# Four-layer network on one core: blocks centred by their weights, row maxima rounded once, new interleaving tables

## Reference

```python
for blk in range(3):
    y = _qlora_linear(h, qweights[i0], scales[i0], biases[i0], lora_a[i0], lora_b[i0])
    y = _layernorm(y, ln_gamma[blk], ln_beta[blk])
    y = gelu(y)
    y = _qlora_linear(y, qweights[i1], ...)
    h = y + h
```

## Time and profile before

| | |
|---|---|
| median of 3 runs | 3338.98 us (3332.05 to 3342.03) |
| profiled execution | 3332.12 us, span 3330.2 us |
| TensorE busy | 2776.6 us, 83%, 20640 products' records |
| ScalarE busy | 1912.7 us, 57% |
| VectorE busy | 1760.9 us, 53% |
| mean granted TensorE clock | 0.851 of 2.4 GHz |
| DMA | 18.83 MB, mean 6 GB/s |

### The profile page before, as it was taken

The page is one execution under the profiler, slowest core; times in us unless marked ns, Lnnn a source line. Parts: engine busy times, 40 slices in busy tenths (PEclk is TensorE's granted clock), DMA queues, the critical chain, the costliest instruction groups (busy, mean ns, idle before and its releaser), DMA issues.

```text
span 3330.2 us, 50269 instructions
## 1 busy us (share of the span) xinstructions
PE 2776.6 (83%) x20640; PEld 1752.4 (53%) x20640; DVE 1760.9 (53%) x2698; ACT 1912.7 (57%) x1963; POOL 3.6 (0%) x13
## 2 busy tenths in 40 slices
PE   7999989778997789977898888987889879897426
PEld 4776556454564545645455554555545545554213
DVE  5464464644656446564555545555455554564425
ACT  2333334875248753587535864468634686347996
POOL 0000000000000000000000000000000000000000
PEclk8998899779997688977999778987779887898558
DMA  3000000000000000000000000000000000000000
GB/s 128 2 1 1 19 2 1 1 1 7 1 1 1 0 8 1 1 1 1 8 2 1 1 1 8 2 1 1 1 4 2 1 1 1 4 1 1 0 0 7
DMA packets 4570, 18.83 MB, mean 6 GB/s; under 512 B 608, under 2 KB 864, under 8 KB 3808
## 3 DMA queue, kind: packets, MB, share of 16 engines
q1 hardware_dynamic: 4320, 15.38, 1.2%
HBM read 13.28 MB, written 2.10 MB: 5 GB/s over the span
## 4 chain that ended last, share of the span: by engine, by line
PE 58%; ACT 19%; DVE 12%; issue 11%; DVEq 0%; DMA 0%; ACTq 0%; SPq 0%
ACT back_cosines L1379 6%; PE two_ps L1934 3%; ACT back_cosines L1381 3%; PE one_ps L918 2%; PE one_ps L1934 2%; PE two_ps L1334 2%; PE one_ps L1220 2%; PE two_ps L966 1%; PE one_ps L1782 1%; PE two_ps L918 1%; ACT L1379 1%; PE one_ps L893 1%; PE two_ps L613 1%; PE one_ps L899 1%; PE one_ps L822 1%
## 5 line engine op out<-in xcount | busy, mean ns | idle before, releaser
L1379 ACT ACTIVATE back_cosines<-back_cosines 128x2048 f32<-128x2048 f32 x256 | 473.3, 1899 | 0.5
L989 ACT ACTIVATE front_scratch<-one_ps 128x1152 f32<-128x1152 f32 x168 | 171.6, 1022 | 230.4 <-PE one_ps L904 230.2
L1934 PEld LDWEIGHTS two_ps<-zero_f,wts 128*128 128x128 f32 x1270 | 210.1, 232 | 114.6 <-issue 90.9
L1934 PE MATMUL two_ps<-zero_f,wts 128*128 128x128 f32 x1270 | 235.2, 327 | 35.1 <-DVE back_cosines L1452 18.1
L1381 ACT ACTIVATE back_cosines<-back_cosines,wts 128x2048 f32<-128x2048 f32 x128 | 252.1, 1994 | 13.3 <-DVE back_cosines L1452 13.1
L853 DVE TENSOR_REDUCE front_negm<-one_ps 128x8 f32<-128x1024 f32 (+1 forms) x168 | 202.5, 1221 | 99.0 <-PE one_ps L828 97.7
L1389 DVE TENSOR_REDUCE back_nsum<-back_cosines 128x8 f32<-128x2048 f32 x64 | 144.4, 2281 | 186.9 <-ACT back_cosines L1379 186.9
L752 ACT ACTIVATE back_cosines<-two_ps,wts 128x512 fp32r<-128x512 f32 x28 | 19.2, 687 | 236.3 <-PE two_ps L966 236.3
L822 PE MATMUL one_ps<-front_qkr 32*128 32x128 f32 (+1 forms) x896 | 117.8, 363 | 42.7 <-issue 34.4
L1452 DVE TENSOR_SCALAR back_cosines<-two_ps 128x2048 f32<-128x2048 f32 x56 | 128.1, 2287 | 30.2 <-PE two_ps L1313 30.1
L989 ACT ACTIVATE back_cosines<-two_ps 128x1152 f32<-128x1152 f32 (+1 forms) x84 | 86.1, 1025 | 98.3 <-PE two_ps L904 98.3
(11 more groups left out here) (635 smaller groups left out, 5941.8 us busy)
## 6 DMA issues: line engine op xcount, KB each, us to landing
wts<-w_dram SPq DMA_DIRECT2D x1, 4184.0 KB, 15.2
front_xin<-x_dram SPq DMA_DIRECT2D x8, 256.0 KB, 4.3
out_dram<-back_z SPq DMA_DIRECT2D x8, 256.0 KB, 2.0
wts<-w_dram SPq DMA_DIRECT2D x1, 1736.5 KB, 19.1
wts<-w_dram SPq DMA_DIRECT2D x1, 1199.0 KB, 5.4
wts<-w_dram SPq DMA_DIRECT2D x1, 1152.0 KB, 16.7
wts<-w_dram SPq DMA_DIRECT2D x3, 256.0 KB, 5.9
wts<-w_dram SPq DMA_DIRECT2D x1, 516.5 KB, 4.5
```

The source lines that it names most:

```text
L989: nc.scalar.activation(h.probs[:, e % 2, 0:n * HEADW].rearrange("p (k c) -> p k c", c=HEADW), h.ps[:, 0:n, 0:HEADW], ACT.Exp, scale=float( ...
L1379: nc.scalar.activation(cosines, cosines, func, scale=scale).then_inc(h.arc_pass.sem, 1)
L1934: nc.tensor.matmul(h.ps[:, bank, quarter * P:(quarter + 1) * P], C("ident"), zero_f[:].broadcast_to([P, P]), start=True, stop=True, skip_g ...
```

## The change

The row maxima are written by the reductions directly in fp32r into the even columns of `negm`. The copies into neighbour columns, the exact two-part split and its constants go. TensorE multiplies each tile by an fp32r identity instead of transposing it in fp32: three tiles after the last reduction but one, the fourth after the last, into a second bank. VectorE copies 384 columns and then 128 into `maxTr`, and the scores wait for the second copy.

In the blocks, the centring is applied to the first linear's weights and bias once, before the loop. ScalarE squares PSUM plus the centred bias, and VectorE's output pass adds that bias and multiplies. The bias add, the centring product and the stage names `block{i}_in` go.

All nine order lists are new. The idle products are placed anew: 91 in a front pass, 96 in a back pass. The load of `qlora` moves ahead of `lora` and the quantised weights and has a semaphore of its own.

The entries of the lists are left out of the diff.

```diff
-    "block0": ("y", "xn", True, "eps5", "block0_in", None),
+    "block0": ("y", "xn", False, "eps5", None, None),
...
-            yield
-            pe.wait_ge(h.max_pair.sem, h.max_pair.at(turn, s))
+            yield from max_end_pe(pe, h, turn, s, MSETS)
+
+        def max_end_pe(pe, h, turn, s, sets):
+            yield
+            pe.wait_ge(h.max_done.sem, h.max_done.at(turn, s, sets - 1))
             for t in range(TILES):
-                last = nc.tensor.transpose(h.ps[:, 0, t * P:(t + 1) * P], h.negm[:, t, :], C("ident"))
-            last.then_inc(h.negm_ps.sem, 1)
+                if t == TILES - 1:
+                    yield
+                    pe.wait_ge(h.max_done.sem, h.max_done.at(turn, s, sets))
+                last = nc.tensor.matmul(h.ps[:, t // (TILES - 1), t % (TILES - 1) * P:(t % (TILES - 1) + 1) * P],
+                                        h.negm[:, t, :], ident_r[:], start=True, stop=True, skip_group_check=True)
+                if t >= TILES - 2:
+                    last.then_inc(h.negm_ps.sem, 1)
...
-        def max_end_dve(dve, h, turn, s, sets):
-            yield
-            dve.wait_ge(h.max_done.sem, h.max_done.at(turn, s, sets))
-            for t in range(TILES):
-                last = nc.vector.tensor_copy(max_columns(h, slice(t, t + 1), 1)[:, 0], max_columns(h, slice(t, t + 1), 0)[:, 0])
-            last.then_inc(h.max_pair.sem, 1)
-            yield
-            dve.wait_ge(h.negm_ps.sem, h.negm_ps.at(turn, s))
-            high_dve(dve, h.ps[:, 0, :], h.high[:, 0, :], "m_sign", h.negm_high)
-            yield
-            dve.wait_ge(h.negm_high.sem, h.negm_high.at(turn, s))
-            split_dve(dve, h.ps[:, 0, :], h.high[:, 0, :], "m_low", h.maxTr[:, :], h.negm_ready)
+        def max_end_dve(dve, h, turn, s):
+            for i, columns in enumerate((slice(0, (TILES - 1) * P), slice((TILES - 1) * P, TOK))):
+                yield
+                dve.wait_ge(h.negm_ps.sem, h.negm_ps.at(turn, s, i + 1))
+                nc.vector.tensor_copy(h.maxTr[:, columns], h.ps[:, i, 0:columns.stop - columns.start]).then_inc(h.negm_ready.sem, 1)
...
-                        pe.wait_ge(h.negm_ready.sem, h.negm_ready.at(turn, s))
+                        pe.wait_ge(h.negm_ready.sem, h.negm_ready.at(turn, s, 2))
...
         def block_pe(pe, h, turn, s):
...
-            yield from norm_pe(pe, h, turn, s)
+            yield
+            pe.wait_ge(h.norm_sq.sem, h.norm_sq.at(turn, s))
+            nc.tensor.matmul(h.ps[:, 1, :], C("mean"), h.sq[:], start=True, stop=True).then_inc(h.norm_var.sem, 1)
...
         def block_act(act, h, turn, s):
             i = int(s[-1])
-            yield from norm_act(act, h, turn, s)
+            yield
+            act.wait_ge(h.lin_ps.sem, h.lin_ps.at(turn, s, 1))
+            nc.scalar.activation(h.sq[:], h.ps[:, 2, :], ACT.Square, bias=centred_bias[:, i:i + 1]).then_inc(h.norm_sq.sem, 1)
+            yield
+            table(LN_EXP)
+            act.wait_ge(h.norm_var.sem, h.norm_var.at(turn, s))
+            nc.scalar.activation(h.sq[:], h.ps[:, 1, :], ACT.Ln, bias=C("eps5")).then_inc(h.norm_ln.sem, 1)
+            yield
+            table(LN_EXP)
+            act.wait_ge(h.norm_ln.sem, h.norm_ln.at(turn, s))
+            nc.scalar.activation(h.sq[:], h.sq[:], ACT.Exp, scale=-0.5).then_inc(h.norm_rstd.sem, 1)
...
         def block_dve(dve, h, turn, s):
...
-            dve.wait_ge(h.lin_ps.sem, h.lin_ps.at(turn, s, 1))
-            nc.vector.tensor_scalar(h.y[:], h.ps[:, 2, :], bias[:, 2 * i:2 * i + 1], None, ALU.add).then_inc(h.resid.sem, 1)
-            yield from norm_dve(dve, h, turn, s)
+            dve.wait_ge(h.norm_rstd.sem, h.norm_rstd.at(turn, s))
+            nc.vector.scalar_tensor_tensor(out=h.xn[:], in0=h.ps[:, 2, :], scalar=centred_bias[:, i:i + 1], in1=h.sq[:],
+                                           op0=ALU.add, op1=ALU.mult).then_inc(h.norm_out.sem, 1)
...
+            load("qlora")
             load("lora")
             sp.dma_start(weff_int[:], qw_dram).then_inc(qint_loaded, 16)
-            load("qlora")
...
         def lora_pe(pe):
...
+            pe.wait_ge(*weights_of("qlora"))
+            last = nc.tensor.matmul(two_back.ps[:, 1, 2 * P:2 * P + 3], C("centre"), W("qlora", "bias")[:, 0:6:2], start=True, stop=True)
...
-                .then_inc(weff_ready, 1)
+                .then_inc(dequant_step, 1)
+            nc.vector.tensor_copy(centred_bias[:], two_back.ps[:, 1, 2 * P:2 * P + 3]).then_inc(dequant_step, 1)
+            dve.wait_ge(dequant_step, 5)
+            first_linear = weff[:].rearrange("p (n c) -> p n c", c=P)[:, 0:6:2, :]
+            nc.vector.tensor_reduce(weff_sum[:], first_linear, AX.X, ALU.add).then_inc(dequant_step, 1)
+            dve.wait_ge(dequant_step, 6)
+            nc.vector.scalar_tensor_tensor(out=first_linear, in0=weff_sum[:].unsqueeze(2).broadcast_to([P, 3, P]), scalar=-1.0 / P,
+                                           in1=first_linear, op0=ALU.mult, op1=ALU.add).then_inc(weff_ready, 1)
...
+            nc.vector.tensor_copy(ident_r[:], C("ident")).then_inc(consts_ready, 1)
```

More of the change, by code:

```diff
@@ L86 @@
 LOADS = {"const": ("const",), "masks": ("masks",), "first": ("causal0",), "moe0": ("moe0",), "front": ("causal1", "mqa", "moe1"),
-         "lora": ("lora",), "back": ("qlora", "linear"), "late": ("causal2", "mlp", "arccos")}
+         "lora": ("lora",), "qlora": ("qlora",), "back": ("linear",), "late": ("causal2", "mlp", "arccos")}
 def columns():
@@ L132 @@
 ORDER = ["load", "causal0", "moe0", "causal1", "mqa", "moe1", "linear", "causal2", "mlp",
-         "arccos", "qlora", "block0_in", "block0", "block1_in", "block1", "block2_in", "block2"]
+         "arccos", "qlora", "block0", "block1", "block2"]
 CAUSAL = ("causal0", "causal1", "causal2")
@@ L349, in __init__ @@
         self.front, self.region, self.passes = parts is FRONT, region, passes
-        if not self.front:
-            stages |= {f"block{i}_in" for i in range(3)}
         norms = [n for kind, n in parts if kind == "norm"] + [n for kind, n in parts if kind == "block"]
@@ L409, in __init__ @@
             parts = scratch[:, 8 * TOK:12 * TOK]
-            self.negm = scratch[:, 12 * TOK:13 * TOK].rearrange("p (t c) -> p t c", t=TILES)
+            self.negm = rounded("negm", [P, TILES, P], 12 * TOK)
             self.y = sb("y", [P, TOK])
@@ L465, in __init__ @@
         self.negm_clear = signal("negm_clear", {"causal2": 1})
-        self.max_pair = signal("max_pair", {s: 1 for s in CAUSAL + ("mqa",)})
-        self.negm_high = signal("negm_high", {s: 1 for s in CAUSAL + ("mqa",)})
-        self.negm_ps = signal("negm_ps", {s: 1 for s in CAUSAL + ("mqa",)})
-        self.negm_ready = signal("negm_ready", {s: 1 for s in CAUSAL + ("mqa",)})
+        self.negm_ps = signal("negm_ps", {s: 2 for s in CAUSAL + ("mqa",)})
+        self.negm_ready = signal("negm_ready", {s: 2 for s in CAUSAL + ("mqa",)})
         self.score_ps = signal("score_ps", {s: CSETS for s in CAUSAL} | {"linear": CSETS, "mqa": QSETS, "arccos": 2 * UNITS})
@@ L848, in max_dve @@
                 if m == 0 and not h.front:
-                    nc.vector.memset(h.negm[:], 0.0).then_inc(h.negm_clear.sem, 1)
+                    nc.vector.memset(h.negm[:].bitcast(F32), 0.0).then_inc(h.negm_clear.sem, 1)
                     dve.wait_ge(h.negm_clear.sem, h.negm_clear.at(turn, s))
                 dve.wait_ge(h.max_ps.sem, h.max_ps.at(turn, s, m + 1))
-                into = max_columns(h, slice(2 * b + qt, 2 * b + qt + 1), 0)[:, 0, js, g0:g0 + ng]
+                into = max_columns(h, 2 * b + qt)[:, js, g0:g0 + ng]
                 nc.vector.tensor_reduce(into, h.ps[:, js, :].rearrange("p j (g k) -> p j g k", k=keys),
                                         AX.X, ALU.max, negate=True).then_inc(h.max_done.sem, 1)
-            yield from max_end_dve(dve, h, turn, s, MSETS)
-        def max_end_dve(dve, h, turn, s, sets):
-            yield
-            dve.wait_ge(h.max_done.sem, h.max_done.at(turn, s, sets))
-            for t in range(TILES):
-                last = nc.vector.tensor_copy(max_columns(h, slice(t, t + 1), 1)[:, 0], max_columns(h, slice(t, t + 1), 0)[:, 0])
-            last.then_inc(h.max_pair.sem, 1)
-            yield
-            dve.wait_ge(h.negm_ps.sem, h.negm_ps.at(turn, s))
-            high_dve(dve, h.ps[:, 0, :], h.high[:, 0, :], "m_sign", h.negm_high)
-            yield
-            dve.wait_ge(h.negm_high.sem, h.negm_high.at(turn, s))
-            split_dve(dve, h.ps[:, 0, :], h.high[:, 0, :], "m_low", h.maxTr[:, :], h.negm_ready)
+            yield from max_end_dve(dve, h, turn, s)
+        def max_end_dve(dve, h, turn, s):
[3 more added lines that the diff above has]
+                nc.vector.tensor_copy(h.maxTr[:, columns], h.ps[:, i, 0:columns.stop - columns.start]).then_inc(h.negm_ready.sem, 1)
         def trio(e):
@@ L1184, in mqa_pe @@
                         last.then_inc(h.max_ps.sem, 1)
-            yield
```

(18 more changed lines are left out.)

26 lines of the change are left out of this document (13 added, 13 removed), and 171 rows, old and new, of tables (ACT_RUNS, DVE_RUNS, IDLE_WORK, PE_RUNS).

## The result

The changed kernel took 3294.45 us, median of four executions (3285.82 to 3303.54), against 3335.52 for the kernel before on the same chip. The ratio is 0.9886, 95% interval 0.9862 to 0.9911: 41 us faster, where 62 were forecast. The profiled execution took 3285.82 us with a span of 3283.9, 46 us under that of before. Repeated later on another chip it took 3308.74 us at a ratio of 0.9919 (0.9888 to 0.995).

What follows compares the result with a forecast made beforehand. No single engine was taken to bound the kernel. Row maxima 37 plus blocks 27 minus 2 once-only gave 62 us off 3332, 3270, forecast as 3277 because the profiled run lay under the median; range 3215 to 3338.

Steps and rivals of the forecast that it cites:

- likeliest case: The prediction's own case: 62 us faster, 3277 us, range 3245 to 3310, chance 0.60.
- The two chains: Last reduction to first scores in causal1: 1.1 us instead of 3.24; block's first product to square: 1.16 instead of 3.13.
- an end at 1.25 and a block at 1.2: Loop: us saved per row-maximum stage end (5 per turn, 30 over six) and per block (3.6 per turn, 22).
- a shorter dependence chain brings its whole length where engines wait for each other: Valuing rule: elsewhere only the removed TensorE work where TensorE is full, nearly nothing where ScalarE is full.
- the added waits hold little: Row maxima: TensorE's two waits for reductions and VectorE's 384-column copy were claimed to delay little.
- third rival: Both edited places lie behind the other half's work and ScalarE: some 20 us gained, 3319 us, chance 0.12.
- I take the balance as zero: New order lists and 544 more idle products: cost and clock gain cancel, bounds -80 to +95 us.
- The second rival: Idle products are the bound on TensorE's queue: 95 us added, 3372 us, 0.11 us per product, chance 0.10.
- A front pass that already leaves TensorE 3 us in 120: First two front passes: TensorE busy 117.0 of 120 us, so added idle products there would lengthen the path.
- The first rival: New products end a third of 500 us at low clock: 82 us less before their cost, 3215 us, chance 0.18.
- A missing one would also cost clock: Argument against slower idle products: present ones, at 0.17 us each, belong to a kernel where removing one loses clock.
- Once only: Preparation of weights before the loop adds 1.5 us at the first turn's wait, and the identity's copy 0.3.

Runs made afterwards that it cites:

- e1: Kernel before with both edits (row maxima and blocks), keeping its old order lists and 119 idle products per turn: 3334.3 us, ratio 1.001.
- e5: Kernel before with both edits, its old order lists and no idle products: 3353.5 us, ratio 1.0062.
- e6: Kernel before without its idle products, nothing else changed: 3340.6 us, ratio 1.0013.
- e8: Changed kernel with the order and idle products of before in the first and last parts, the new ones in the loop: 3258.1 us, ratio 0.9781.
- e11: Changed kernel run again unchanged, on the chip of the hybrid beside it: 3308.74 us, ratio 0.9919 to the kernel before.

## Why the prediction came out as it did

The direction and the range were right: 3294 in 3215 to 3338, and inside the likeliest case's 3245 to 3310. It was 17 us too low (32 for the repeat), and the working is right in fewer places than the total suggests. That the total came near is partly luck: too high a price for the edits was made up by a term that had been put at zero.

- **The two chains.** Lengths right: 0.86 us for 1.1, 1.16 for 1.16. Their worth in the last part comes out in e1, 8.3 us for 7, though most squares there come later than I reckoned, so the agreement may be luck. In the loop it failed. I valued an end at 1.25 and a block at 1.2, 8.6 us per turn, and e1 shows 2.8 at an equal clock. The step that failed is "a shorter dependence chain brings its whole length where engines wait for each other", together with "the added waits hold little": I followed what an instruction depends on, and not what is issued ahead of it on its engine. Under the old lists the first block's square waits 4.17 us with and without the edit, behind moe1 on ScalarE; the scores of causal0 and causal2 come no earlier, or 0.3 us earlier, behind other work and idle products on TensorE. That is the third rival (*covered*) for the old order. I had read the blocks' worth from the last part, where no front half stands between.
- **What removed work does to the clock** was left out. I counted 0.65 us of TensorE work saved per end and 0.9 per block as gain. With both edits the low clock is 71 us longer with idle products (e1 against before) and 82 longer without (e5 against e6). That removed work is the reason is likely and not proven.
- **"I take the balance as zero".** This term was mis-sized, and it is where the time came from. The new order and the products placed for it brought -30 to -41 us (e1 at 1.001 against after at 0.9919 and 0.9886), within my bounds of -80 to +95. It holds opposite terms, read from the profiles: -12.6 per turn in the loop (408.1 to 395.5), +24 in the first part and +14 in the last (both against e8).
- **The second rival** was right in its place. "A front pass that already leaves TensorE 3 us in 120" was its argument, and a longer first part its sign. The first part got longer, by 0.13 us per product, and by 9 us for the order, which no rival had. I priced it for the whole run or not at all, when each part of the program has its own answer.
- **The first rival** was right in its mechanism, not in its size: 120 to 190 us of low clock ended, where it supposed 165. By the slope within one kernel, 0.3 us per us and not 0.5, that is an estimated 36 to 57 us where it wanted 82. Its sign, a mean clock above 0.90, did not come.
- **"A missing one would also cost clock"** is right, and worth almost nothing: e6 has 353 us more of low clock and at most 0.3% more time.
- Once only: 0.9 us for 1.5. ScalarE's busy time: 0.2 us apart. Mean clock 0.878, within 0.84 to 0.88.

The Trainium skill ("TensorE: Matmul & The Clock Gate", Terms) puts the penalty of the lower clock at half the throttled time. For e6 that would be an estimated 176 us; the runs show 4 to 8, net of what the left-out products had cost. Within one kernel the price is mostly 0.3 to 0.4, not 0.5. That part of the low clock lies where TensorE isn't waited for would explain it; of the low clock of a turn of before, 73 to 82 us lie in the arccos stretch.

What stays open: how much of the loop's 11 us needs the edits. The new lists have no steps for the old chains, and the old kernel wasn't run under them. That the first block's square comes 1.2 us after its product only under the new order suggests that the edits have a share in it. Nor was it settled which entries of the new order bring what.

## What to carry to other kernels

Before you price a shortened chain, look at what is issued ahead of its next instruction on that engine, at every place where it occurs: here a block's square came no earlier, with a shorter chain, until the order let it. Read the clock beside the time when you take work from TensorE; here both edits left it lower. Idle products were worth 0.6 to 1.0% in the order they were placed for, cost 5 us a turn in one they were not placed for, and cost 0.13 us each in a part where TensorE was already full. When one table serves a prologue, a loop and an epilogue, price and choose it for each; here the split was worth another 1.1%.

## What the hardware showed

The same loop turn of the same execution can take 396 or 413 us. Two turns of the changed kernel's second profile (e11), one behind the other, with the same instructions:

```profile
1624.30:2020.50 396.20, 353.86 (x2708) 233.03 (x2708) 213.04 (x316) 239.64 (x246) 0.00 (x0) 0.89 0.01 3
2020.50:2433.20 412.70, 373.75 (x2709) 243.92 (x2708) 213.93 (x316) 239.73 (x246) 0.00 (x0) 0.84 0.01 2
```

ScalarE and VectorE do the same work in the same time. Only the clock differs, 0.89 and 0.84, which is 85 and 133 us at 1.2 GHz, and TensorE's busy time grows by 20 us. So the granted clock is not fixed by the program alone, and a difference of 10 us between two single profiles says nothing here unless the low clock beside it is the same.
